# Two layers of a macaron transformer on one core: the last FFN phase is entered from within the second attention

## The chip, the cores and the metric

One core of a Trainium2 chip runs the whole program. The metric is the device time of one execution in microseconds (us), lower is better; the figure compared is the median over executions. TensorE is PE in the profile (its weight loads PEld), VectorE is DVE, ScalarE is ACT, GpSimd is POOL, and SyncE (SP) issues the DMAs.

## The reference

Input x has 2 batches of 1024 tokens of 256 features, all in f32. A "macaron" layer is half an FFN, an attention, half an FFN, each added to x. Layer 0 has 16 heads of 16 with rotary positions, layer 1 has 16 query heads of 128 that share 4 key/value heads; its FFN is six blocks deep.

```
x = x + 0.5 * L0_ffn(norm(x)); x = x + L0_attn(norm(x)); x = x + 0.5 * L0_ffn(norm(x))
x = x + 0.5 * L1_ffn(norm(x)); x = x + L1_attn(norm(x)); x = x + 0.5 * L1_ffn(norm(x))
L1_ffn: six times  x = gelu(x @ W1.T + b1) @ W2.T + b2 + x,  and after each but the last  x = norm(x) * g + b
L1_attn: q, k, v = x @ Wq.T, x @ Wk.T, x @ Wv.T; per head softmax(causal(q @ k.T)) @ v; all heads @ Wo.T + bo
```

## The kernel before

**Precision.** Each f32 operand of a product is kept as a high part (a copy rounded to the matmul type) and a low part (the difference), and a product is three matmuls, low by high, high by low, high by high (`PARTS`). So nearly every tensor is written twice: a high part by ACT (a Copy) and a low part by DVE or POOL (a subtraction); code and text call this a split.

**Phases.** The 2048 tokens are four chunks of 512 (chunks 0 and 1 are batch 0, chunks 2 and 3 are batch 1). Phase 0 is the FFN of layer 0, then comes attention 0, phases 1 and 2 are the two FFNs before attention 1, and phase 3 is the last FFN, six blocks of four chunks. Each engine has its own program, an endless straight order with semaphore waits: an instruction that waits holds up everything behind it on that engine.

**A step of an FFN** is one chunk in one block. For each of eight hidden tiles j, PE does `mm1(j)` (6 matmuls, L291), ACT the gelu (L351) and the high part (L357), DVE the low part (`low(j)`, L462), and PE, three tiles later, `pe_second` (12 matmuls, L316). Beside it DVE takes the former chunk's result (`dve_take`, L388), normalises it (`dve_norm`: statistics L417 and L422, three Newton steps for the inverse root L431 to L434, and the normalised rows `xn` L445), PE turns `xn` (8 transposes, `pe_transpose_chunk`, L277), ACT scales the turned tile and takes its high part (`act_affine`, L337 and L342), DVE its low part (`dve_low_input`, L454), and POOL adds the bias row for the residual (`pool_xb`, L524 to L529). Weights of the next block are loaded into `wraw` and split by quarters, one in each step.

**Attention 1** has 32 head turns (2 batches by 16 heads) in 8 groups of four; groups 0 to 3 are batch 0. The order in a head is a table of words for each engine (`ORDER`, L612): `s6` is the score of query tile 6, `max6` its maximum on DVE (L837), `exp6` its exponential on ACT (L797), `t` the transposes of the probabilities (L732), `high` and `low` the two parts of these (L805, L848), `m` the product with the values (L745), `c` the context, `wo` the output projection (L772) which DVE adds to x (`add_head`, L881). `k`, `v`, `q` are projections (L756); k and v stand only in a group's last head, for the next group. A prime means the next head, a minus the head before. Projections, value transposes and `wo` all use one PSUM bank (`MISC_PS`), in turn: PE fills it, ACT and DVE read it, and only then (`misc_free`) can PE fill it again. Query tiles of one head are all scored before its probabilities for the second half of the keys are turned: `t4` waits for `exp7`.

**Weights of attention 1** lie in HBM in ten pieces for each group. SP loads them into `xb` (L1393, L1397), POOL splits them (`pool_split_a1`, L903 and L905). For the first group this load waits until the FFN before it has written its last input (`xT_ready`).

**Entry into phase 3.** When the last head is added, every engine meets: ACT takes the high parts of the four weight quarters (`entry_high`, L543), DVE and POOL two low parts each (`entry_low`, L548), DVE does the statistics of all 16 token tiles, the Newton steps and the rows of the four chunks in turn; PE turns each, ACT and DVE split each; only then, behind all four chunks in PE's order (`pre_posts`), comes `mm1(0)` of chunk 0.

## Time and profile before

| | |
|---|---|
| median of 3 executions | 2781.11 us (2776.45 to 2782.05) |
| the profiled execution: its own time, its span | 2773.37 us, 2771.5 us |
| busy share of PE, PEld, DVE, ACT, POOL | 91%, 76%, 67%, 51%, 13% |
| granted clock of PE, mean | 0.959 of full |

The busy share says which engine the kernel as a whole leans on. A stage is read from the timeline instead: instructions of one engine in order of time, each line with its start, its length, and in brackets how long the engine had been idle before it and which instruction's end released it.

### The profile page before, as it was taken

What the parts mean: (1) busy time and instruction counts of PE and PEld (TensorE: products, weight loads), DVE (VectorE), ACT (ScalarE), POOL (GpSimd) and SP (SyncE); (2) the same over time, 40 slices, a digit from 0 to 9 for tenths busy, and PEclk for the clock granted to TensorE, in tenths of its full rate; (3) what the DMA queues carried; (4) which work ended last, traced back from release to release, by engine and by line L of the source; (5) the groups of instructions that cost most, each with busy time, mean ns of one, the idle gap of its engine ahead of it and who ended that gap; (6) DMA issues with size and microseconds to landing.
All of it is one profiled execution on the core that took longest, in us unless ns stands there. A gap on an engine that the chain in (4) does not pass through costs nothing. (4 is left out here: it accounts for less than half of the span.)

```text
span 2771.5 us, 49967 instructions
## 1 busy us (share of the span) xinstructions
PE 2532.7 (91%) x16744; PEld 2115.2 (76%) x16744; DVE 1846.5 (67%) x4006; ACT 1399.9 (51%) x2466; POOL 360.4 (13%) x277
## 2 busy tenths in 40 slices
PE   3985989869999999996999999999999599999999
PEld 3863444358888888884887877878878588888888
DVE  4566777457567777764766766767777666777773
ACT  3430555645455555542655555555555455555553
POOL 1000000011122222103000010010000212222220
PEclk9986899979999999997999999999999799999999
DMA  4026133000000000001000000000000000000000
GB/s 155 0 80 141 25 48 47 2 31 31 1 31 31 0 30 30 0 1 38 1 20 1 19 19 0 19 19 0 19 23 9 31 22 9 31 31 0 30 0 31
DMA packets 18925, 73.21 MB, mean 26 GB/s; under 512 B 3328, under 2 KB 8192, under 8 KB 15616
## 3 DMA queue, kind: packets, MB, share of 16 engines
q1 hardware_dynamic: 18816, 71.78, 9.1%
q8 instruction: 66, 1.08, 0.2%
q14 instruction: 43, 0.35, 0.0%
HBM read 61.02 MB, written 10.49 MB: 26 GB/s over the span
## 5 line engine op out<-in xcount | busy, mean ns | idle before, releaser
L316 PEld LDWEIGHTS ps<-w,hid 128*128 128x128 f32 x5376 | 698.9, 191 | 53.6 <-DVE rb L388 15.3
L316 PE MATMUL ps<-w,hid 128*128 128x256 f32 x5376 | 719.2, 284 | 0.6 <-DVE hid L462 0.5
L291 PE MATMUL ps<-xT,w 128*128 (+1 forms) x2688 | 705.7, 399 | 0.0
L462 DVE TENSOR_TENSOR hid<-gel,hid 128x512 fp32r<-128x512 f32 x448 | 397.2, 897 | 368.2 <-ACT hid L357 359.4
L351 ACT ACTIVATE gel<-ps,b 128x512 f32<-128x512 f32 x448 | 306.9, 686 | 560.3 <-issue 547.2
L291 PEld LDWEIGHTS ps<-xT,w 128*128 128x128 f32 x2688 | 481.0, 191 | 79.7
L357 ACT ACTIVATE hid<-gel 128x512 fp32r<-128x512 f32 x448 | 272.8, 622 | 0.0
L745 PE MATMUL ps<-pT,v_sb 128*128 128x512 f32 (+3 forms) x1152 | 260.3, 357 | 1.3 <-DVE pT L848 1.3
L718 PE MATMUL ps<-k_sb,q_sb 128*128 128x512 f32 (+3 forms) x1152 | 251.4, 351 | 1.5 <-DVE q_sb L865 1.4
L837 DVE TENSOR_REDUCE negmax<-ps 128x1 f32<-128x128 f32 (+7 forms) x256 | 192.3, 751 | 78.6 <-PE ps L721 77.5
L1287 DVE TENSOR_REDUCE nmx<-ps 128x1 f32<-128x512 f32 (+3 forms) x384 | 196.0, 552 | 73.0 <-PE ps L1158 55.3
L805 ACT ACTIVATE pT<-ps 128x512 fp32r<-128x512 f32 (+3 forms) x384 | 178.0, 489 | 109.5 <-PE ps L732 109.5
L848 DVE TENSOR_TENSOR pT<-ps,pT 128x512 fp32r<-128x512 f32 (+3 forms) x384 | 205.5, 549 | 24.7 <-ACT pT L805 22.6
L718 PEld LDWEIGHTS ps<-k_sb,q_sb 128*128 128x128 f32 x1152 | 192.6, 190 | 26.8 <-DVE q_sb L865 1.8
L526 POOL TENSOR_TENSOR xb<-xn,rows 128x1024 f32 (+1 forms) x40 | 102.9, 2571 | 791.5 <-DVE xn L445 791.5
L1254 ACT ACTIVATE pT<-ps 128x1024 f32<-128x1024 f32 (+1 forms) x192 | 145.3, 811 | 119.2 <-PE ps L1158 81.9
L756 PE MATMUL ps<-xT,w_a 128*128 (+1 forms) x576 | 162.0, 417 | 44.9 <-DVE k_sb L865 15.4
L745 PEld LDWEIGHTS ps<-pT,v_sb 128*128 128x128 f32 x1152 | 182.7, 189 | 24.7 <-issue 7.3
L454 DVE TENSOR_TENSOR xT<-xTf,xT 128x1024 f32 (+1 forms) x64 | 135.9, 2124 | 86.7 <-ACT xT L342 86.7
L277 PE MATMUL ps<-ident,xn 128*128 128x128 f32 x512 | 82.6, 313 | 117.1 <-DVE xn L445 97.3
L277 PEld LDWEIGHTS ps<-ident,xn 128*128 128x128 f32 x512 | 65.5, 160 | 130.3 <-DVE xn L445 86.6
L797 ACT ACTIVATE p_hi<-ps,negmax 128x640 f32<-128x640 f32 (+3 forms) x128 | 122.4, 956 | 83.3 <-DVE negmax L837 80.9
(111 smaller groups left out, 2909.6 us busy)
## 6 DMA issues: line engine op xcount, KB each, us to landing
wraw<-in_wffn SPq DMA_DIRECT2D x11, 2048.0 KB, 7.8
xb<-in_w_a SPq DMA_DIRECT2D x8, 1280.0 KB, 5.4
qk_dram<-rope_hl SPq DMA_DIRECT2D x16, 512.0 KB, 3.0
xT<-qk_dram SPq DMA_DIRECT2D x60, 128.0 KB, 8.2
xb<-in_wffn SPq DMA_DIRECT2D x3, 2048.0 KB, 10.5
qk_own<-qk_dram SPq DMA_DIRECT2D x36, 128.0 KB, 6.4
x<-in_x SPq DMA_DIRECT2D x4, 512.0 KB, 5.5
rot<-in_rot SPq DMA_DIRECT2D x1, 2048.0 KB, 18.5
```

Source lines behind the costliest of these rows:

```text
L291: last = nc.tensor.matmul(ps[:, HPS + j % 4, :], w[par][:, wp, 0, k * HIDDEN + j * PART:k * HIDDEN + (j + 1) * PART], xT[:, xp, k, bass.ds ...
L316: last = nc.tensor.matmul(y_ps[:, t, :], hid[:, hp, j % 4, t * PART:(t + 1) * PART], w[par][:, wp, 1, j * DIM:(j + 1) * DIM], start=j == 0 ...
L351: nc.scalar.activation(gel[:, j % 4, :], ps[:, HPS + j % 4, :], ACT.Gelu, bias=b1[:, bass.ds((p.tab + blk) * HT + j, 1)]).then_inc(gelu_do ...
L357: nc.scalar.activation(hid[:, 0, j % 4, :], gel[:, j % 4, :], ACT.Copy).then_inc(round_done, 1)
L462: nc.vector.tensor_tensor(hid[:, 1, j % 4, :], gel[:, j % 4, :], hid[:, 0, j % 4, :].bitcast(f32), ALU.subtract).then_inc(low_done, 1)
L718: last = nc.tensor.matmul(dst, q_sb[:, h % 2, qp, q], k_sb[:, kp, k], start=x3 == 0, stop=x3 == 2 and not diagonal)
L745: last = nc.tensor.matmul(ps[:, AV_PS, cols], v_sb[:, vp, kt, :], pT[:, pp, m % PT_SLOTS, cols], start=kt == 0 and n == 0, stop=kt == 3 + ...
L756: last = nc.tensor.matmul(ps[:, MISC_PS, :], a1_piece(wp, which, h, k), xT[:, xp, k, bass.ds(b * SEQ + half * CHUNK, CHUNK)], start=first, ...
L805: nc.scalar.activation(pT[:, 0, m % PT_SLOTS, q0 * PART:], ps[:, T_BANKS[m % 2], q0 * PART:], ACT.Copy).then_inc(pt_high, 1)
L837: nc.vector.tensor_reduce(negmax[:, h % 2, qt:qt + 1], score_view(qt), AX.X, ALU.max, negate=True).then_inc(max_ready, 1)
L848: nc.vector.tensor_tensor(pT[:, 1, m % PT_SLOTS, q0 * PART:], ps[:, T_BANKS[m % 2], q0 * PART:], pT[:, 0, m % PT_SLOTS, q0 * PART:].bitcas ...
L1287: nc.vector.tensor_reduce(nmx[:, g % 2, at:at + 1], src[:, 0:width], AX.X, ALU.max, negate=True)\
```

## The change

1. **Batch 0 enters during the last group.** Groups 4 to 7 only add to batch 1, so chunks 0 and 1 of x are final by then. Their normalisation (8 tiles) is put between DVE's instructions of heads 0 to 2 of the last group (`closing_items`), and their transposes go where the unused `k` words of heads 1 and 2 stand (`transpose_early`, item `n`), through the shared bank: PE 4 transposes, ACT a copy, DVE a subtraction, four times in all. For phase 3's entry there is no scale and shift (they are 1 and 0), so the high part is copied from PSUM at once. A semaphore of its own, `xn_early`, counts the two chunks.
2. **The weights of the first block** are loaded into `wraw` instead of `xb`. ACT takes two quarters before its `high` 10 of the last head and two after the last context; POOL takes all four low parts. PE's first `mm1` waits for two quarters, its first `pe_second` for all.
3. **Batch 1 enters during FFN chunks 0 and 1.** Its statistics, Newton steps and rows (`dve_late_norm`) stand between the `low(j)` of chunk 0, the second chunk's rows in chunk 1; the turns are at the end of chunk 0 and behind `pe_second(0)` of chunk 1. The first block's chunks are written out, not looped. `dve_entry` and `pre_posts` are empty for phase 3.
4. **The weights of attention 1** go through `wraw` too, and the first load waits only for the split of the last weights of phase 2. SBUF is laid out anew for both attentions, with `p_lo` and `p_hi` packed to the triangle that is used, so that `w` of block 0 lies over tensors that are free early.

```diff
+                if p.k == 3 and isinstance(blk, int) and blk == 0:
+                    for c in range(1, CHUNKS):
+                        step(at(blk, c, par, kind), at(blk, c - 1, par, kind))
+                    return
                 with engine.Fori(1, CHUNKS) as c:
...
-            pe.wait_ge(w_split, 4 * (p.n0 + blk + 1))
+            opening = first_block(p, at)
+            if opening and c == 0:
+                pe.wait_ge(w_split, 4 * p.n0 + 2)
+            else:
+                pe.wait_ge(w_split, 4 * (p.n0 + blk + 1))
...
+                if opening and c == 0 and j == LAG:
+                    pe.wait_ge(w_split, 4 * (p.n0 + 1))
                 if j >= LAG:
                     pe_second(pe, at, j - LAG)
                 elif prev is not None:
                     pe_second(pe, prev, HT - LAG + j)
+                if opening and c == 1 and j == LAG:
+                    pe_transpose_chunk(pe, p.s0 - 1)
+            if opening and c == 0:
+                pe_transpose_chunk(pe, p.s0 - 2)
             if prev is not None and prev[5] != "final":
                 pe_transpose_chunk(pe, prev[1])
 
...
+                if first_block(p, at) and (c, j) in ((0, HT), (1, 5)):
+                    act_affine(act, p.s0 - EARLY + c, EARLY + c, 0)
                 if j == HT and prev is not None and prev[5] != "final":
...
+                if not early:
+                    wait(dve, tr_ready, s + chunk)
+                elif chunk:
+                    dve.wait_ge(misc_ready, uses(GROUPS - 1, "n", chunk, 2 * chunk - 1) + 1)
 
                 if not isinstance(xb_made, int) or xb_made > 0:
                     wait(dve, xb_ready, xb_made + chunk)
...
+            parts, late, opening = [], [], first_block(p, at)
+            if opening and c < 2:
+                if c == 0:
+                    late_norm.extend(dve_late_norm(dve, p))
+                late = late_norm[:-1] if c == 0 else late_norm[-1:]
             if prev is not None and prev[5] != "final":
                 parts = dve_norm(dve, prev[1], prev[2], prev[5] == "inner", xb_before(p, prev),
-                                 prev[1] - (CHUNKS - 1) * p.entries)
...
                 low(j)
+                if late and (c == 0 or j == 0):
+                    late.pop(0)()
+                if opening and (c, j) == (1, 5):
+                    dve_low_input(dve, p.s0 - 1, EARLY + 1)
                 if j == 4 and splits_next(p, kind):
                     dve_split(dve, p, at)
                 if j == 1 and prev is not None:
...
         def dve_entry(dve, p):
 
-            if not p.pre:
+            if not p.pre or p.k == 3:
                 return
             s = p.s0 - CHUNKS
...
 
-        def entry_high(act, p):
-            if p.pre:
-                x_ready(act, p.k)
-                act.wait_ge(w_loaded, 16 * (p.n0 + 1))
-                for q in range(4):
-                    nc.scalar.activation(quarter(w[p.n0 % 2][:, 0], q), quarter(xb_raw, q), ACT.Copy).then_inc(w_high, 1)
+        def entry_raw(p):
+            return wraw if p.k == 3 else xb_raw
+
+        def entry_high(act, p, quarters=range(4)):
+            act.wait_ge(w_loaded, 16 * (p.n0 + 1))
+            for q in quarters:
+                nc.scalar.activation(quarter(w[p.n0 % 2][:, 0], q), quarter(entry_raw(p), q), ACT.Copy)\
+                    .then_inc(w_high, 1)
 
...
 
-        def in_order(engine, heads, first=0, last=GROUP):
+        EARLY_AT = (1, 2)
+
+        def in_order(engine, heads, first=0, last=GROUP, closing=None):
 
             todo = []
             for h in heads:
                 for word in ORDER[engine].split():
                     item = word.strip("'-0123456789")
+                    if item == "k" and closing is not None and h - closing in EARLY_AT:
+                        todo.append(("n", h, 2 * (h - closing - EARLY_AT[0]) + int(word.strip("'k"))))
+                        continue
                     head = h + word.count("'") - word.count("-")
                     of_group = {"k": 0, "v": 0, "w": 0}.get(item, head % GROUP)
                     if first <= head < last and head % GROUP == of_group:
...
+            group = [items(e, GROUPS - 1 + over) for over in (-1, 0)]
+            closing = closing_items(e, engine)
+            for item, head, n in in_order(engine, range(GROUP + 1), -1, GROUP, 0):
+                for at in [at for at in closing if at == (item, head, n)]:
+                    closing.pop(at)()
+                group[head // GROUP + 1][item](head % GROUP, n)
+            assert not closing
+
+        def closing_items(e, engine):
+
+            p = phase(3)
+            if engine == "act":
+                return {("high", 3, 10): lambda: entry_high(e, p, (0, 1))}
+            if engine == "dve":
+                norm = dve_early_norm(e, p)
+
+                def begin():
+                    e.wait_ge(misc_free, A1_MISC * (GROUPS - 2))
+                    norm[0]()
+                return {("max", 0, 6): begin, ("max", 0, 7): norm[1], ("low", 0, 3): norm[2], ("low", 0, 6): norm[3],
+                        ("low", 0, 8): norm[4], ("max", 1, 1): norm[5], ("max", 2, 1): norm[6]}
...
+            def transpose_early(h, n):
+                c, k = n // KD, n % KD
+                pe.wait_ge(xn_early, c + 1)
+                wait(pe, misc_free, uses(i1, "n", h, n))
+                for t in range(TPC):
+                    last = nc.tensor.transpose(ps[:, MISC_PS, t * PART:(t + 1) * PART],
+                                               xn[:, t, k * PART:(k + 1) * PART], ident[:])
+                last.then_inc(misc_ready, 1)
+
             def transpose_values(h, r):
...
 
-            return dict(exp=exp, high=high, c=ctx_part,
+            def early(h, n):
+                c, k = n // KD, n % KD
+                act.wait_ge(misc_ready, uses(i1, "n", h, n) + 1)
+                nc.scalar.activation(xT[:, 0, k, c * CHUNK:(c + 1) * CHUNK], ps[:, MISC_PS, :], ACT.Copy)\
+                    .then_inc(misc_high, 1)
...
-            return dict(max=maximum, inv=inverse, low=low, c=ctx_part, v=take_values, wo=add_head,
+            def early(h, n):
+                c, k = n // KD, n % KD
+                cols = slice(c * CHUNK, (c + 1) * CHUNK)
+                dve.wait_ge(misc_high, A1_HIGHS * i1 + HIGHS[which_group(i1)]["n", h, n] + 1)
+                nc.vector.tensor_tensor(xT[:, 1, k, cols], ps[:, MISC_PS, :], xT[:, 0, k, cols].bitcast(f32),
+                                        ALU.subtract).then_inc(misc_free, 1)
...
+
+        a1_raw = wraw_flat.rearrange("p (n e) -> p n e", e=DIM)
 
         def pool_split_a1(pool, i, first):
 
             wait_apart(pool, (w1_loaded, 16 * (i + 1)))
             for piece in range(10):
-                cols = slice(piece * DIM, (piece + 1) * DIM)
+                tile, at = (w_kvq, piece) if piece < 6 else (w_o1, piece - 6)
+                cols = slice(at * DIM, (at + 1) * DIM)
                 if not first:
                     wait_apart(pool, (misc_ready, A1_MISC * (i - 1) + last_use(piece)))
...
                 if k == 3:
-                    sp.wait_ge(xT_ready, S_ATT[1])
-                    sp.dma_start(xb[:, 0:10, :], a["w_a1"][0, :, :].rearrange("p (t e) -> p t e", e=DIM))\
+                    sp.wait_ge(w_split, 4 * p.n0)
+                    sp.dma_start(a1_raw[:, 0:10, :], a["w_a1"][0, :, :].rearrange("p (t e) -> p t e", e=DIM))\
                         .then_inc(w1_loaded, 16)
                     with sp.Fori(1, GROUPS) as i:
...
-                    load(p.n0, p.tab, xb_raw)
+                    load(p.n0, p.tab)
                 if k == 1:
                     load(p.n0 + 1, 1)
...
+                if k == 3:
+                    for c in range(EARLY):
+                        pool.wait_ge(xn_early, c + 1)
+                        pool_residual(pool, c)
                 if p.pre:
-                    entry_low(pool, nc.gpsimd, p, (2, 3) if k == 3 else range(4))
+                    entry_low(pool, nc.gpsimd, p, range(4))
                 if k == 3:
-                    pool.wait_ge(w_split, 4 * (p.n0 + 1))
-                    pre_posts(pool, k, lambda p, s, c: pool_xb(pool, s, c, None, None))
+                    for c in range(EARLY, CHUNKS):
+                        pool_xb(pool, p.s0 - CHUNKS + c, c, None, None)
                 walk(p, pool, lambda at, prev: pool_step(pool, p, at, prev))
                 pool_post(pool, p, tail(p))
...
                     act.wait_ge(xT_ready, S_ATT[1])
                     attention(act, "act", act_att)
-                entry_high(act, p)
+                    act.wait_ge(av_done, 12 * GROUP * GROUPS)
+                    entry_high(act, p, (2, 3))
+                if p.pre and k != 3:
+                    x_ready(act, k)
+                    entry_high(act, p)
                 pre_posts(act, k, lambda p, s, c: act_affine(act, s, c, 0))
```

The order on the engines, at three places.

DVE, head 0 of the last group, from `wo2` of the head before to `low` 2 and 3 (`negmax` is `max6`, then `max7`). Before:

```order
L881 SCALAR_TENSOR_TENSOR x<-ps,rowinv,x 128x256 [waits inv_ready,misc_ready]
L881 SCALAR_TENSOR_TENSOR x<-ps,rowinv,x 128x256
L848 TENSOR_TENSOR pT<-ps,pT 128x512 [waits pt_high]
L837 TENSOR_REDUCE negmax<-ps 128x1 [waits s_ready]
L881 SCALAR_TENSOR_TENSOR x<-ps,rowinv,x 128x256 [waits inv_ready,misc_ready]
L881 SCALAR_TENSOR_TENSOR x<-ps,rowinv,x 128x256
L848 TENSOR_TENSOR pT<-ps,pT 128x384 [waits pt_high]
L837 TENSOR_REDUCE negmax<-ps 128x1 [waits s_ready]
```

With the change, from the same `low` 0 on:

```order
L952 TENSOR_TENSOR pT<-ps,pT 128x512 [waits pt_high]
L452 BN_STATS stats<-x 128x6 [waits misc_free]
L452 BN_STATS stats<-x 128x6 x7
L941 TENSOR_REDUCE negmax<-ps 128x1 [waits s_ready,dve_link,in_loaded]
L985 SCALAR_TENSOR_TENSOR x<-ps,rowinv,x 128x256 [waits inv_ready,misc_ready]
L985 SCALAR_TENSOR_TENSOR x<-ps,rowinv,x 128x256
L952 TENSOR_TENSOR pT<-ps,pT 128x384 [waits pt_high]
L457 BN_AGGR mv<-stats 128x2 x8
L459 TENSOR_SCALAR var<-mv 128x8 [waits dve_link]
L460 TENSOR_SCALAR nt<-var 128x8 [waits dve_link]
L462 TENSOR_SCALAR rstd<-nt 128x8 [waits dve_link]
L941 TENSOR_REDUCE negmax<-ps 128x1 [waits s_ready,dve_link]
```

Eight statistics stand ahead of `max6` and eleven short instructions ahead of `max7`.

PE, head 1 of the last group, from the end of `s7` to the first projection; this is new, before there was nothing between `s7` and `m0` nor between `t3` and `q0`:

```order
L812 MATMUL ps<-mask_b,ident_b 128x128
L857 MATMUL ps<-ident,xn 128x128 [waits misc_free,xn_early]
L857 MATMUL ps<-ident,xn 128x128 x3
L835 MATMUL ps<-pT,v_sb 128x512 [waits ctx_low,pt_low]
L835 MATMUL ps<-pT,v_sb 128x512 x2
L822 MATMUL ps<-ident,p_lo 128x128 [waits pt_low]
L822 MATMUL ps<-ident,p_lo 128x128
L822 MATMUL ps<-ident,p_lo 128x128 [waits pt_low]
L857 MATMUL ps<-ident,xn 128x128 [waits misc_free,xn_early]
L857 MATMUL ps<-ident,xn 128x128 x3
L846 MATMUL ps<-xT,w_kvq 128x512 [waits misc_free,w1_split]
L846 MATMUL ps<-xT,w_kvq 128x512 x5
```

Two fillings of the shared bank come ahead of the projection, each behind a wait for the one before.

PE, from the last `wo` to the first matmuls of phase 3. Before:

```order
L772 MATMUL ps<-w_a,ctxT 128x256 x5
L277 MATMUL ps<-ident,xn 128x128 [waits aff_done,xn_ready]
L277 MATMUL ps<-ident,xn 128x128 x7
L277 MATMUL ps<-ident,xn 128x128 [waits aff_done,xn_ready]
L277 MATMUL ps<-ident,xn 128x128 x7
L277 MATMUL ps<-ident,xn 128x128 [waits aff_done,xn_ready]
L277 MATMUL ps<-ident,xn 128x128 x7
L277 MATMUL ps<-ident,xn 128x128 [waits aff_done,xn_ready]
L277 MATMUL ps<-ident,xn 128x128 x7
L291 MATMUL ps<-xT,w 128x512 [waits gelu_done,xT_ready,w_split]
```

With the change:

```order
L871 MATMUL ps<-w_o,ctxT 128x256 x5
L318 MATMUL ps<-xT,w 128x512 [waits gelu_done,xT_ready,w_split]
L318 MATMUL ps<-xT,w 128x512 x5
L318 MATMUL ps<-xT,w 128x512 [waits gelu_done]
L318 MATMUL ps<-xT,w 128x512 x5
L318 MATMUL ps<-xT,w 128x512 [waits gelu_done]
L318 MATMUL ps<-xT,w 128x512 x5
L318 MATMUL ps<-xT,w 128x512 [waits gelu_done]
L318 MATMUL ps<-xT,w 128x512 x5
L349 MATMUL ps<-w,hid 128x256 [waits y_free,low_done,w_split]
```

The 32 transposes are gone from between the two stages.

## Rows read from the trace of the kernel before

**Rows 1.** Windows: busy us (count) of PE, PEld, DVE, ACT, POOL, PEclk, DMA share, GB/s
```profile
2081.50:2105.10 23.60, 23.60 (x154) 20.50 (x153) 17.98 (x41) 13.94 (x33) 0.00 (x0) 1.00 0.00 1
2030.00:2056.90 26.90, 23.26 (x129) 18.63 (x128) 14.33 (x29) 11.57 (x24) 1.13 (x2) 1.00 0.00 0
2177.60:2193.30 15.70, 7.45 (x32) 6.31 (x33) 9.47 (x15) 7.51 (x9) 8.90 (x4) 0.50 0.11 46
```

**Rows 2.** Timeline of PE at phase 3's entry: start us, length us, instruction [idle before <- releaser]
```profile
2160.77 0.95 PE L772 MATMUL ps<-w_a,ctxT 128*128 128x256 f32 x6 [1.01 <-issue]
...
2193.32 7.64 PE L291 MATMUL ps<-xT,w 128*128 128x512 f32 x24
...
2201.48 1.70 PE L316 MATMUL ps<-w,hid 128*128 128x256 f32 x12 [0.52 <-DVE hid L462]
```

**Rows 3.** Timeline of ACT: weight quarters, the switch to gelu
```profile
2162.67 3.90 ACT L543 ACTIVATE w<-xb 128x1024 fp32r<-128x1024 f32 x4 [4.67 <-DVE x L881]
...
2197.62 1.28 ACT L351 ACT_TABLE_LOAD   x1
...
2198.92 1.26 ACT L351 ACTIVATE gel<-ps,b 128x512 f32<-128x512 f32 x2
```

**Rows 4.** Timeline of POOL at the entry into attention 1
```profile
1282.81 10.23 POOL L1434 TENSOR_TENSOR x<-x,rows 128x1024 f32<-128x1024 f32 x4 [79.84 <-DVE xn L445]
1296.44 0.40 POOL L903 CAST w_a<-xb 128x256 fp32r<-128x256 f32 x1 [3.40 <-DMA xb<-in_w_a]
```

**Rows 5.** Groups by line and form, 2162.6 to 2193.4 us: busy us, mean ns
```profile
L417 DVE BATCH_NORM_STATS2 stats<-x 128x6 f32<-128x256 f32 x16 | 5.3, 410 | 0.0
...
L422 DVE BATCH_NORM_AGGREGATE mv<-stats 128x2 f32<-128x6 f32 x16 | 1.2, 144 | 0.0
```

**Rows 6.** Timeline of DVE and POOL in the entry
```profile
2165.69 4.64 POOL L548 TENSOR_TENSOR w<-xb,w 128x1024 fp32r<-128x1024 f32 x2 [92.40 <-ACT w L543]
2168.08 4.47 DVE L548 TENSOR_TENSOR w<-xb,w 128x1024 fp32r<-128x1024 f32 x2
...
2174.29 0.17 DVE L431 TENSOR_TENSOR nt<-rstd 128x16 f32<-128x16 f32 x1
...
2176.18 1.38 DVE L445 TENSOR_SCALAR xn<-x,mv,rstd 128x256 f32<-128x256 f32 x4
```

**Rows 7.** Timeline of PE, DVE and ACT, head 0 of the last group: max6, s7's end, max7, exp7, t4
```profile
2071.31 1.08 DVE L837 TENSOR_REDUCE negmax<-ps 128x1 f32<-128x896 f32 x1
...
2073.17 0.23 PE L721 MATMUL ps<-mask_b,ident_b 128*128 128x128 bf16 x1
...
2073.56 1.21 DVE L837 TENSOR_REDUCE negmax<-ps 128x1 f32<-128x1024 f32 x1
...
2074.85 1.12 ACT L797 ACTIVATE p_hi<-ps,negmax 128x1024 f32<-128x1024 f32 x1
...
2076.89 1.06 PE L732 MATMUL ps<-ident,p_hi 128*128 128x128 f32 x8
```

**Rows 8.** Timeline of ACT and PE: the shared bank from a fill's end to the next; four transposes
```profile
2043.21 0.60 ACT L826 ACTIVATE k_sb<-ps 128x512 fp32r<-128x512 f32 x1 [1.30 <-PE ps L756]
...
2044.59 1.66 PE L756 MATMUL ps<-xT,w_a 128*128 x6 [1.41 <-DVE k_sb L865]
...
2062.33 0.60 PE L765 MATMUL ps<-ident,xTf 128*128 128x128 f32 x4
```

**Rows 9.** Timeline of ACT at the end of the last head: high10, the last context
```profile
2154.72 0.39 ACT L805 ACTIVATE pT<-ps 128x256 fp32r<-128x256 f32 x1 [0.43 <-PE ps L732]
...
2157.40 0.60 ACT L814 ACTIVATE ctxT<-ps 128x512 fp32r<-128x512 f32 x1 [1.59 <-PE ps L745]
```

**Rows 10.** Timeline of PE in phase 3: a step's end with its 8 transposes
```profile
2237.35 1.09 PE L277 MATMUL ps<-ident,xn 128*128 128x128 f32 x8
2238.20 1.64 PE L291 MATMUL ps<-xT,w 128*128 x6
```

**Rows 11.** DMA issues, 2000 to 2300 us: count, KB each, median us to landing
```profile
wraw<-in_wffn SPq DMA_DIRECT2D x2, 2048.0 KB, 7.8
```

127 lines of the change are left out of this document (76 added, 51 removed).

## The prediction

> **What bounds the kernel now.** I read the page first, then the windows. In a plain head of attention 1 PE is busy for the whole of its 23.6 us while DVE works 18.0 and ACT 13.9 of them [rows 1]: in there PE sets the time, and DVE has some 5.6 us of idle time in a head. The seam between attention 1 and phase 3 is different. The PE timeline shows the last `wo` ending at 2160.77 + 0.95 = 2161.72 and the first `mm1` at 2193.32 [rows 2]: 31.6 us in which PE does nothing but 32 transposes. In the second half of that seam PE's granted clock is 0.50, which is 1.2 GHz of 2.4 [rows 1], after PE had stood still from 2161.72 on. The clock is still recovering when `mm1` starts, and `pe_second` follows 8.16 us later [rows 2]. A second, smaller seam lies at the entry into attention 1: POOL ends its bias sums at 1282.81 + 10.23 = 1293.04, then idles 3.40 us for the weights' DMA, and PE's first projection waits for the split behind it [rows 4].
>
> **The change, part by part.** All is set against the profiled execution (2773.4 us, of which the span is 2771.5); its time is 7.7 us under the median, and I take the same difference off the median.
>
> *Removed, the seam: 31.6 us.* PE's order goes from the last `wo` straight to `mm1(0)`. What it waits for: two weight quarters. ACT's four quarters took 3.90 us, 0.98 each [rows 3]; POOL's subtraction is 4.64 / 2 = 2.32 each [rows 6]. ACT starts them ahead of `high10`, at about 2154.3, so POOL has two done at about 2155.3 + 4.6 = 2160, before the last `wo` ends; the last two are done some 2.9 us after 2161.72, and `pe_second(0)` wants them 5.8 us after it. So this wait costs nothing; without that cover it would cost up to 4.6.
>
> *Removed, the slow start: 2.1 us.* The chain before `pe_second(0)` is one `mm1` (1.64, rows 10 show such a six), then from the table load to the product 2201.48 - 2197.62 = 3.86 us [rows 2, 3], 5.5 together. Four `mm1` at full clock are about as long. I take 5.8, and 0.3 more because the statistics of batch 1 (8 x 0.33 = 2.7) now stand between `low(0)` and `low(1)`: 8.16 - 6.1 = 2.1. The rows put the gelu 1.30 us behind the start of the table load [rows 3]. The Trainium skill (ScalarE: Activation LUTs, What ACT_TABLE_LOAD costs) adds a drain of about 1.38 us to a load of 1.28; the trace does not show that drain, and by the page the opening would be 1.4 us longer and the whole gain smaller by as much.
>
> *Removed at the entry of attention 1: 3.4 us.* The DMA is issued a block earlier, so POOL's 3.40 us of idle time [rows 4] go. Everything behind (k projection, value projection) only moves forward.
>
> *Added in head 0 of the last group: 3.8 us.* Ahead of `max6` and `max7` DVE gets 2.7 (8 statistics, 5.3 / 16 each) and 8 x 0.08 + 3 x 0.21 = 1.2 [rows 5]; 0.21 is the pitch of a short instruction, (2176.18 - 2174.29) / 9 for the nine of the Newton steps [rows 6]. DVE runs without a gap there, and `t4` on PE waits for `exp7`, which waits for `max7`: `exp7` ends at 2075.97, `t4` starts at 2076.89, so the cover is 0.9 [rows 7]. 3.9 - 0.9 = 3.0 reach PE. The first Newton step (0.6) and the later `exp7` push the low part of q's first half, and the second half waits for the shared bank: 0.8 more. PE has no slack in a head [rows 1], so nothing of this is made up later.
>
> *Added, the early turns: 3.8 us in each of heads 1 and 2, 7.6 together.* The bank's turnaround, from ACT's copy to the next filling, is 2044.59 - 2043.21 = 1.38, and four transposes take 0.60 [rows 8]. Two turns are 2 x (0.60 + 1.38) = 4.0 behind the end of `s7`. On DVE both stand ahead of `max7`, on ACT ahead of `exp6` and `exp7`. So `exp7` ends about 4.0 + 1.2 + 1.3, with hand-overs some 6.9, behind the end of `s7`, and `t4` about 7.3 behind it; before it was 2076.89 - 2073.40 = 3.5 [rows 7]. That the stretch with k and v has the same chain and shows PE busy 23.3 of 26.9 us [rows 1] speaks for stalls of this kind.
>
> *Added, Newton steps 2 and 3 and the rows: 2.5 us.* On DVE 2 x 0.6 and 2 x 1.38 [rows 6] make 4.0. They stand near idle time of DVE; I let 2.5 reach PE.
>
> *Added at the end of the last head: 0.7 us.* Two quarters (1.95) stand ahead of `high10`. ACT was idle 0.43 before it and 1.59 before the last context [rows 9], which hides most of it.
>
> *Moved into the FFN: 2.2 us.* 16 transposes in two lots of 8, 1.09 each lot [rows 10], on PE, where nothing covers them. The statistics, Newton steps, rows and two low inputs of batch 1 are about 2.7 + 1.2 + 1.9 + 2.8 and two subtractions of 1.2 (the second of L548's, rows 6: 4.47 less the wait behind POOL) on DVE, over two chunks; `low(j)` is wanted three tiles after `mm1(j)`, and I cost them at nothing beyond the 0.3 above. SP's load of block 1's weights is issued when POOL is done and lands 7.8 us later [rows 11], about when ACT's split in chunk 0 asks for it; a microsecond of lateness there is hidden by the three-tile lag. POOL's two early bias sums (some 2.6 each, 10.23 / 4, rows 4) run beside attention and are awaited by nobody.
>
> Sum: 31.6 + 2.1 + 3.4 = 37.1 less 3.8 + 7.6 + 2.5 + 0.7 + 2.2 = 16.8 is a gain of **20.3 us**: 2753.1 for the profiled execution, **2761** for the median. Bounds of the costs: below, only the turns' own PE time (4 x 0.60) and the 2.2, so 4.6 and a gain of 32.5 (2749). Above, four bank turns at 2.0, all DVE work of the early norm (2.7 + 1.2 + 1.9 + 2.8), 2.0 for ACT's quarters, 2.2, and 6.3 for an opening that is late on POOL and the DMA: 27 and a gain of 10 (2771). I take the middle because the order puts the pieces ahead of `max6`, `max7`, where DVE has no gap.
>
> **Rivals.**
>
> *The norm hides (2754.5).* DVE idles 5.6 us in a head [rows 1] and its 8.6 us of early norm are spread over three heads. If all of it hides, 3.8 + 2.5 = 6.3 less is paid. For it: the idle share. Against: DVE's idle time lies elsewhere in the head, not between `max5` and `low3`. 15%.
>
> *POOL stands in DVE's way at the opening (2768).* The row of the seam shows it: DVE's two weight subtractions started at 2168.08 and took 4.47, while POOL ran two until 2170.33 [rows 6]. The first DVE one lasted as long as POOL's, the second 1.2. With the change POOL subtracts four quarters, 9.3 us, and makes two bias sums of 2.6 in the first two chunks, beside DVE's `low(j)`, which also reads two SBUF tensors. If the last quarter reaches into `low(0)` (2.3) and both sums hold `low(j)` up to PE (2 x 2.6), the opening costs 7.5 us more. For: the row. Against: POOL should be done 2 us before `low(0)`, which comes some 4.9 us after 2161.72, and `low(j)` has the three-tile lag. The Trainium skill (SBUF — State Buffer, SBUF: two separate sides) has the rule: a DVE op with two SBUF inputs and a GpSimd op that reads SBUF take one port pair in turn, for the whole instruction. The row agrees. 12%.
>
> *Half clock in the last group (slower, up to 2807).* PE granted 0.50 after it had stood still [rows 1]. The change puts waits of 1 to 4 us into a group that had none. Each microsecond at 1.2 GHz costs half of one, so the gain is gone when over 40.6 us of the last group (some 92, not quite four heads of 23.6) run at half clock, and if all do it is 46 - 20 = 26 slower. Against: the stretch with k and v has stalls of up to 1.4 us and shows 1.00 [rows 1, 8]. 3%.
>
> *The seam is only shifted (no change).* If the early turns or the last weight quarter came so late that PE stood still for some 20 us again, somewhere between the last `wo` and chunk 1. The weights' load is issued when POOL has split the last group's weights, early in that group, and no instruction that is moved is that long. 2%.
>
> **How the numbers follow.** The forecast has 68%. The likeliest is 2761. The range goes from the lower bound of the costs, 2749, to 2770, which takes in the late opening; it leaves out the clock and the shifted seam and the outermost runs. A measurement of this kernel tells about 0.2% (5.6 us) from no change: faster by more than that is 68 + 15 + 12 = 95%, within it 2%, slower 3%.
>
> **What would show it.** In the profile of the changed kernel: (1) the last `wo` and the first `mm1` less than 1 us apart, `pe_second` 5.5 to 6.5 us later at a granted clock of 1.00; (2) POOL's first split of attention 1 right behind its bias sums; (3) the last group about 14.6 us longer than its 92, in three lots: idle time of PE before L822 and L846 (`t4`, projections) in heads 0, 1 and 2; (4) steps of chunks 0 and 1 as long as the others but for 1.1 us of transposes. The forecast is wrong if the last group grows by under 8 or over 20 us, if PE waits for `w_split` at the seam, or if chunk 0 or 1 takes over 3 us more than chunk 2.

## The result, and the profile after

The changed kernel takes 2767.69 us (median of 12 executions, 2751.26 to 2780.14) beside 2779.18 us (12, 2771.89 to 2792.64): a ratio of 0.9943 (interval 0.9918 to 0.9967), or some 16 us less (9 to 23); the two medians themselves are 11.5 us apart. It is faster, and 2767.69 lies in the range of the prediction, 2749 to 2770, 6.7 us above its number. The profiled execution took 2771.37 us (span 2769.5, mean granted clock 0.956), only 2.0 less than that of before. The two timelines, laid side by side from the start, tell why:

| stretch, PE's timeline | before | after | difference |
|---|---|---|---|
| start to the last transposes ahead of attention 1 | 1282.79 | 1299.23 | +16.44 |
| from there to the first projection | 15.00 | 11.53 | -3.47 |
| groups 0 to 6 | 770.34 | 770.44 | +0.10 |
| last group: heads 0, 1, 2 | 23.71, 23.61, 23.61 | 28.39, 27.52, 27.06 | +4.68, +3.91, +3.45 |
| head 3, to the end of the last `wo` | 22.66 | 23.83 | +1.17 |
| last `wo` to the first `pe_second` | 39.76 | 6.23 | -33.53 |
| from there to the end | 570.02 | 575.27 | +5.25 |

All that the change touches gives -18.44 us. The first line arises in attention 0, of which the change moves only the place in memory: PE's first product of its heads starts at 227.2 and 227.8 us, and its last output projection ends at 565.7 and 582.1. Experiments 10 to 12 are about it. In the windows (columns as in [rows 1]) of the last group's four heads and of the opening:

```profile
2081.20:2109.60 28.40, 25.94 (x155) 22.03 (x155) 24.43 (x74) 13.79 (x33) 3.51 (x3) 0.94 0.20 75
2109.60:2137.10 27.50, 25.26 (x162) 21.58 (x162) 20.40 (x47) 14.93 (x35) 2.39 (x1) 1.00 0.00 1
2137.10:2164.20 27.10, 25.10 (x163) 21.55 (x163) 19.31 (x43) 15.07 (x35) 0.00 (x0) 1.00 0.00 1
2164.20:2188.00 23.80, 19.81 (x125) 16.87 (x124) 15.49 (x37) 13.98 (x26) 7.58 (x4) 0.96 0.00 1
2188.00:2194.20 6.20, 6.20 (x25) 4.72 (x24) 1.64 (x4) 3.96 (x6) 1.79 (x1) 0.88 0.53 172
```

Where a head was all PE [rows 1], PE now stands still for 2.0 to 2.5 us in each of heads 0 to 2. The timelines of DVE, ACT and PE show how it comes about in head 0, where [rows 7] had no gap:

```profile
2084.39 2.70 DVE L452 BATCH_NORM_STATS2 stats<-x 128x6 f32<-128x256 f32 x8
2087.18 1.09 DVE L941 TENSOR_REDUCE negmax<-ps 128x1 f32<-128x896 f32 x1
...
2088.97 0.55 DVE L952 TENSOR_TENSOR pT<-ps,pT 128x384 fp32r<-128x384 f32 x1
...
2088.31 1.01 ACT L895 ACTIVATE p_hi<-ps,negmax 128x896 f32<-128x896 f32 x1 [4.12 <-DVE negmax L941]
...
2089.58 0.33 PE L822 MATMUL ps<-ident,p_lo 128*128 128x128 f32 x1 [2.12 <-DVE pT L952]
2089.68 2.16 PE L846 MATMUL ps<-xT,w_kvq 128*128 128x512 f32 x6
```

The statistics push `max6`, for which ACT waits 4.12 us, and everything behind it on DVE. PE's 2.12 us are for `low1` (L952), which stands behind the statistics, `max6` and an addition of `wo3`; ACT had its high part long before (2083.71 to 2084.19). The six matmuls behind take 2.16 us where they take 1.64 at full clock. In head 1 PE waits in the turns themselves, for the one shared bank (L857 is the early turn):

```profile
2116.81 0.63 PE L857 MATMUL ps<-ident,xn 128*128 128x128 f32 x4 [0.49 <-DVE xT L994]
2118.94 1.64 PE L846 MATMUL ps<-xT,w_kvq 128*128 128x512 f32 x6 [1.50 <-DVE xT L994]
```

Then the seam. [Rows 2] had 31.6 us here; now the FFN's first product stands right behind the last `wo`:

```profile
2186.38 1.62 PE L871 MATMUL ps<-w_o,ctxT 128*128 128x256 f32 x6 [1.01 <-issue]
2187.80 6.56 PE L318 MATMUL ps<-xT,w 128*128 128x512 f32 x24
2194.23 1.66 PE L349 MATMUL ps<-w,hid 128*128 128x256 f32 x12
```

That last `wo` took 0.95 before and takes 1.62 now. The windows show a granted clock of 0.53, which is nearly all at the lower level (0.5, 1.2 GHz), and before it PE busy for 0.90 and 0.98 of 2 us:

```profile
2182.00:2184.00 2.00, 0.90 (x6) 0.76 (x6) 0.64 (x4) 0.98 (x2) 2.00 (x2) 1.00 0.00 0
2184.00:2186.00 2.00, 0.98 (x6) 0.77 (x6) 1.00 (x4) 1.50 (x2) 2.00 (x2) 1.00 0.00 0
2186.00:2188.00 2.00, 1.62 (x7) 1.65 (x8) 0.28 (x1) 0.00 (x0) 2.00 (x2) 0.53 0.00 0
2188.00:2190.00 2.00, 2.00 (x8) 1.52 (x7) 0.88 (x2) 0.00 (x0) 1.79 (x1) 0.62 0.00 0
```

Last, chunk 1 of the FFN, in the timelines of DVE, POOL and PE: beside POOL's sum of 2.40 us DVE's low part takes 2.25 and not 0.69, DVE's take (L423) is late, and PE waits for it; at the chunk's end it waits again, for the norm's rows. The last three lines are the first `mm1` of chunks 1, 2 and 3: chunk 1 takes 28.01 us, chunk 2 23.75.

```profile
2217.03 2.25 DVE L500 TENSOR_TENSOR hid<-gel,hid 128x512 fp32r<-128x512 f32 x1 [0.84 <-ACT hid L390]
2219.21 1.27 DVE L423 TENSOR_TENSOR rb<-ps,xb 128x512 f32<-128x512 f32 x2
...
2216.33 2.40 POOL L568 TENSOR_TENSOR xb<-xn,rows 128x1024 f32<-128x1024 f32 x1 [6.98 <-DVE xn L483]
...
2220.03 1.67 PE L349 MATMUL ps<-w,hid 128*128 128x256 f32 x12 [1.50 <-DVE rb L423]
...
2235.56 1.09 PE L300 MATMUL ps<-ident,xn 128*128 128x128 f32 x8 [1.66 <-DVE xn L483]
...
2208.40 1.65 PE L318 MATMUL ps<-xT,w 128*128 128x512 f32 x6
...
2236.41 1.65 PE L318 MATMUL ps<-xT,w 128*128 128x512 f32 x6
...
2260.16 1.65 PE L318 MATMUL ps<-xT,w 128*128 128x512 f32 x6
```

### The profile page after: what moved, and what is told of

It is laid out like the page before. It is cut to its first block and busy times, and to the rows that moved or that the text cites. A ratio compares the mean times of both kernels' runs of the same rounds, so it can differ in the third digit from the quotient of the medians.

```text
span 2769.5 us, 49771 instructions
## 1 busy us (share of the span) xinstructions
PE 2550.3 (92%) x16744; PEld 2123.4 (77%) x16744; DVE 1843.1 (67%) x4018; ACT 1396.5 (50%) x2464; POOL 367.1 (13%) x279
## 5 line engine op out<-in xcount | busy, mean ns | idle before, releaser
L952 DVE TENSOR_TENSOR pT<-ps,pT 128x512 fp32r<-128x512 f32 (+3 forms) x384 | 205.8, 550 | 24.7 <-ACT pT L903 22.7
L809 PEld LDWEIGHTS ps<-k_sb,q_sb 128*128 128x128 f32 x1152 | 192.8, 190 | 26.8 <-DVE q_sb L969 1.8
L846 PE MATMUL ps<-xT,w_kvq 128*128 (+1 forms) x576 | 162.6, 418 | 44.5 <-DVE k_sb L969 15.3
L492 DVE TENSOR_TENSOR xT<-xTf,xT 128x1024 f32 (+1 forms) x62 | 128.9, 2079 | 80.1 <-ACT xT L375 80.1
L300 PE MATMUL ps<-ident,xn 128*128 128x128 f32 x496 | 76.9, 305 | 94.3 <-DVE xn L483 81.0
L846 PEld LDWEIGHTS ps<-xT,w_kvq 128*128 128x128 f32 x576 | 103.7, 193 | 77.1 <-issue 36.1
```

Source lines behind the costliest of these rows:

```text
L809: last = nc.tensor.matmul(dst, q_sb[:, h % 2, qp, q], k_sb[:, kp, k], start=x3 == 0, stop=x3 == 2 and not diagonal)
L846: last = nc.tensor.matmul(ps[:, MISC_PS, :], a1_piece(wp, which, h, k), xT[:, xp, k, bass.ds(b * SEQ + half * CHUNK, CHUNK)], start=first, ...
L952: nc.vector.tensor_tensor(pT[:, 1, m % PT_SLOTS, q0 * PART:], ps[:, T_BANKS[m % 2], q0 * PART:], pT[:, 0, m % PT_SLOTS, q0 * PART:].bitcas ...
```

## The experiments

Each is read by the same stretches as above: the four heads of the last group, from `t0` to `t0` on PE (head 3 to the end of the last `wo`), from `t0` of head 3 to the first `pe_second`, and from there to the end. All times in us, one profile each.

| kernel | heads 0, 1, 2, 3 | `t0` of 3 to `pe_second` | to the end |
|---|---|---|---|
| before | 23.71, 23.61, 23.61, 22.66 | 62.42 | 570.02 |
| changed | 28.39, 27.52, 27.06, 23.83 | 30.06 | 575.27 |
| 1 turns at vacant places | 28.23, 23.61, 24.43, 24.34 | 30.72 | 575.01 |
| 2 norm spread | 23.83, 23.62, 28.46, 29.33 | 36.33 | 574.51 |
| 3 both | 23.66, 23.60, 24.43, 24.10 | 30.74 | 574.83 |
| 4 load late | 28.22, 28.91, 27.06, 23.82 | 30.11 | 575.07 |
| 5 late rows | 28.51, 27.51, 27.06, 23.84 | 30.11 | 573.83 |
| 6 no sums | 28.43, 27.50, 27.08, 23.83 | 30.07 | 573.44 |
| 7 quarters last | 28.42, 27.53, 27.07, 23.10 | 32.25 | 575.43 |
| 8 end filled | 28.41, 27.50, 27.06, 22.82 | 25.46 | 578.15 |
| 9 all moves | 23.68, 23.62, 24.42, 24.14 | 26.77 | 572.62 |
| 10 before, again | 23.68, 23.62, 23.59, 22.64 | 62.41 | 570.01 |
| 11 all moves, again | 23.67, 23.61, 24.44, 24.15 | 26.78 | 572.53 |
| 12 changed, again | 28.22, 28.94, 27.06, 23.86 | 29.95 | 575.00 |

**1. The turns at vacant places.**

```diff
-        EARLY_AT = (1, 2)
+        EARLY_AT = dict(pe={(2, "w0'"): 0, (2, "w1'"): 1, (3, "q1'"): 2, (3, "w0'"): 3},
+                        act={(3, "w0"): 0, (3, "w1"): 1, (3, "q1'"): 2, (4, "w0"): 3})
+        EARLY_AT["dve"] = {(3, "w0"): 0, (3, "w1"): 1, (4, "q1"): 2, (4, "w0"): 3}
...
-                        ("low", 0, 8): norm[4], ("max", 1, 1): norm[5], ("max", 2, 1): norm[6]}
+                        ("low", 0, 8): norm[4], ("max", 1, 1): norm[5], ("inv", 3, 0): norm[6]}
```

> The changed kernel, with the four early turns of batch 0 taken out of the places of k0' and k1' in heads 1 and 2 (ahead of exp6 and max7) and put where the shared bank has a vacant place: w0' and w1' ahead of head 3, q1' and w0' in head 3. The norm's DVE pieces stay where they were, only the second rows stand later, in head 3. In the changed kernel the last group takes 106.8 us from the first t0 to the end of the last wo, and its heads are 4.7, 3.9, 3.5 and 1.2 longer than before. Theory A (the place costs): the turns are dear because exp7 and t4 of their head wait for two bank turnarounds in a row; at vacant places only PE's own 4 x 0.6 = 2.4 us is paid, heads 1 and 2 lose some 5.5 us together, and the last group takes 101 us. Theory B (the work costs, wherever it stands: four fillings of the shared bank of 1.4 and more): the last group stays at 106 to 107.5 us and the cost moves to head 3.

Measured: the last group takes 100.6 us (101 expected by A, 106 by B). Head 1 is a plain head again, though the first rows still stand just before it. Heads 2 and 3 pay 0.8 and 0.5 for what PE itself does in the turns. Times: 0.9916 of before (0.9884 to 0.9949).

**2. The norm where DVE is idle.**

```diff
-        EARLY_AT = (1, 2)
+        EARLY_AT = (2, 3)
...
-                return {("max", 0, 6): begin, ("max", 0, 7): norm[1], ("low", 0, 3): norm[2], ("low", 0, 6): norm[3],
-                        ("low", 0, 8): norm[4], ("max", 1, 1): norm[5], ("max", 2, 1): norm[6]}
+                return {("max", 0, 4): begin, ("q", 1, 0): norm[1], ("max", 1, 4): more_variance,
+                        ("q", 2, 0): norm[3], ("max", 2, 4): both, ("max", 3, 4): norm[5]}
```

> The changed kernel, with the early norm of batch 0 cut into lots of at most 2.0 us, each put where the trace of before shows DVE idle: ahead of max4 (2.13 idle there, 1.53 in head 0) and of q0' (0.94), spread over all four heads; the turns stay at the places of k0' and k1', but in heads 2 and 3, as the norm is done later. Theory A (the place costs): the 4.7 us of head 0 go nearly (0.5 left), head 1 is a plain head plus 0.5, head 2 carries the turns as head 1 did (3.9), head 3 has no q projections and pays some 3 us for its turns; the last group takes 101 to 102 us in place of 106.8. Theory B (DVE's 8.6 us of added work cost wherever they stand): 106 us or more.

Measured: head 0 is 23.83, 0.1 over before's, and head 1 23.62: what stands of the norm in these two heads is hidden. That is A, but the group takes 105.2 and not 101 to 102, since heads 2 and 3, to which the turns moved, are 4.9 and 6.7 longer than before's (with half clock in both, and in head 3 the weight quarters of experiment 7). In head 3 PE has no q projections to do meanwhile, so it waits for ACT and DVE, and then gets half clock (timeline and window):

```profile
2162.68 0.91 PE L854 MATMUL ps<-pT,v_sb 128*128 128x256 f32 x6 [2.35 <-DVE pT L971]
```
```profile
2164.00:2168.00 4.00, 3.44 (x15) 2.65 (x14) 2.06 (x3) 1.42 (x3) 0.00 (x0) 0.51 0.00 0
```

Had only the total been looked at (-1.6 us), theory B (106 or more) would have seemed nearly right; the heads one by one say the reverse. Times: 0.9919 (0.9889 to 0.9948).

**3. Both.** The edits of 1 and 2 together, with the norm's last pieces ahead of `q0'` in head 2 and of `inv0` in head 3.

> Both moves together: the norm's pieces ahead of max4 and q0', the turns at the vacant places of w0', w1' ahead of head 3 and of q1', w0' in head 3. Theory A (the place costs, and the two costs are independent, so they add): PE pays its own 2.4 us of transposes, the end with its 1.2 us and about 1 us of leftovers, so the last group takes 97.5 to 99 us against 106.8, and the kernel is some 8 us faster than the changed one, 24 faster than before. Theory B (the work costs): 105 us or more.

Measured: 95.8 us, 2.2 over before's 93.6 and 1.7 under the lowest that was expected. It saves 11.0 us, more than experiments 1 and 2 together (6.2 and 1.6), as the turns no longer meet the places that made them dear in 2. Of the 2.2, PE's own part of a turn is some 0.4 (head 2 with two of them is 0.82 longer), less than the 0.6 of its row, and 0.36 is half clock in the last `wo` (1.31 against 0.95 in [rows 2]). These are all the idle times of PE in the group; only the 0.30 ahead of a turn (L874, for the shared bank) has no counterpart in the kernel before:

```profile
2138.22 0.91 PE L852 MATMUL ps<-pT,v_sb 128*128 128x256 f32 x6 [0.30 <-DVE pT L969]
2141.14 1.00 PE L852 MATMUL ps<-pT,v_sb 128*128 128x512 f32 x3 [0.59 <-DVE pT L969]
2147.93 0.63 PE L874 MATMUL ps<-ident,xn 128*128 128x128 f32 x4 [0.30 <-DVE x L1002]
2151.84 0.96 PE L888 MATMUL ps<-w_o,ctxT 128*128 128x256 f32 x6 [1.41 <-DVE ctxT L977]
2153.82 1.31 PE L888 MATMUL ps<-w_o,ctxT 128*128 128x256 f32 x6 [1.01 <-issue]
```

So of 13.2 us some 11 were the places; the 2.2 left are the work and that half clock. Times: 0.9897 (0.9874 to 0.9920).

**4. The first load late.**

```diff
-                    sp.wait_ge(w_split, 4 * p.n0)
+                    sp.wait_ge(xT_ready, S_ATT[1])
                     sp.dma_start(a1_raw[:, 0:10, :], a["w_a1"][0, :, :].rearrange("p (t e) -> p t e", e=DIM))\
```

> The changed kernel, but the weights of attention 1's first group are loaded as before, after xT of the phase is ready, and not a block earlier. Theory A (the term of 3.4 in the prediction): POOL stands idle some 3.4 us behind its bias sums again, and from the start of the last transposes ahead of attention 1 to the first projection it is 15.0 us in place of 11.5. Rival (the 3.5 us gained there come from the new place of the weights in the memory, since w_kvq now lies elsewhere and a1_raw is read in place of xb): it stays at 11.5 us.

Measured: 1312.54 to 1327.38, 14.84 us, with POOL's idle time back; so the term is the load. POOL's timeline, to set beside [rows 4]:

```profile
1312.56 10.22 POOL L1548 TENSOR_TENSOR x<-x,rows 128x1024 f32<-128x1024 f32 x4 [79.97 <-DVE xn L483]
1326.04 0.40 POOL L1017 CAST w_kvq<-wraw 128x256 fp32r<-128x256 f32 x1 [3.26 <-DMA wraw<-in_w_a]
```

Its times, 0.9915 (0.9893 to 0.9937), are no higher than the changed kernel's: executions differ too much for a term of 3 us, which only the timeline shows.

**5. The late rows behind the take**, and **6. POOL's sums cut short** (from 1024 columns to 8; this kernel leaves out most of the residual and bias of chunks 2 and 3).

```diff
-                if late and (c == 0 or j == 0):
+                if late and c == 0:
                     late.pop(0)()
...
                     dve_take(dve, p, prev)
+                    if late:
+                        late.pop(0)()
```

> The changed kernel, but in chunk 1 DVE makes the second half of the late rows behind its take of chunk 0's output and not ahead of low(1). In the changed kernel it is 575.3 us from the first pe_second to the end of the span, 5.2 more than before; a sum of POOL (2.40 us) that is released by these rows runs beside DVE's low(1), which took 2.25 us in place of 0.69, the take is late, and PE waits 1.50 us for it. Theory A (it is the place): the stall of 1.5 goes and the stretch takes 573.7 us. Theory B (the sum then meets the next low(j) and the wait only moves): 575.0 to 575.5 us.

```diff
+                nc.gpsimd.tensor_tensor(xb[:, bass.ds(c * TPC, 1), 0:8], xn[:, 0:1, 0:8], rows[:, B2_1:B2_1 + 1, 0:8],
+                                        ALU.add).then_inc(xb_ready, 1)
```

> The changed kernel with POOL's two bias sums of batch 1 (chunks 2 and 3 of the FFN's first block) cut from 1024 columns to 8, so the residual and bias of these chunks are left out; all instructions and waits stay. Theory A (POOL and DVE take turns at SBUF): low(j) beside them takes 0.69 us and not 2.25 and 2.85, the stall of 1.50 us ahead of pe_second in chunk 1 goes, and the stretch from the first pe_second to the end takes 573 to 573.8 us against 575.3. Rival (DVE's own added norm work or the two lots of transposes make all of the 5.2): 575.0 us or more, and low(j) is as slow as in the changed kernel.

Measured: 573.83 and 573.44, both by A. With the rows behind the take, low(1) and the take (L423) are on time; with POOL's sum at 0.20 us they are so too, in the old order:

```profile
2221.95 0.69 DVE L500 TENSOR_TENSOR hid<-gel,hid 128x512 fp32r<-128x512 f32 x1 [2.13 <-ACT hid L390]
2222.56 1.28 DVE L423 TENSOR_TENSOR rb<-ps,xb 128x512 f32<-128x512 f32 x2
```
```profile
2210.75 0.69 DVE L500 TENSOR_TENSOR hid<-gel,hid 128x512 fp32r<-128x512 f32 x1 [0.84 <-ACT hid L390]
2211.36 1.28 DVE L423 TENSOR_TENSOR rb<-ps,xb 128x512 f32<-128x512 f32 x2
...
2210.05 0.20 POOL L582 TENSOR_TENSOR xb<-xn,rows 128x8 f32<-128x8 f32 x1 [9.16 <-DVE xn L483]
```

So the sum beside the low part made the 1.5 us: moving the rows that release it gets 1.4 us back, removing both sums 1.8. (The 2.85 us of the expectation are a row of two low parts, beside the first sum; no wait of PE came of them.)

**7. All quarters last.**

```diff
-                return {("high", 3, 10): lambda: entry_high(e, p, (0, 1))}
...
-                    entry_high(act, p, (2, 3))
+                    entry_high(act, p)
```

> The changed kernel with all four weight quarters on ACT behind the last context of attention 1 and none ahead of high10. By the prediction's term the two quarters ahead of high10 cost 0.7 us at the end of the last head: without them head 3 takes 23.1 us in place of 23.8; but POOL has its second quarter only some 5.7 us behind ACT's start, so that the first mm1 waits 1.4 us for it, and from the start of t0 in head 3 to the first pe_second it is 30.5 to 31.5 us against 30.06. Rival (the quarters hide fully behind ACT's idle time): head 3 stays at 23.8 us and the first mm1 comes 1.4 us or more later.

Measured: head 3 takes 23.10 us, 0.73 less, the size of the prediction's term (0.7). But the first `mm1` waits 1.59 us for POOL's second quarter, and the four behind it take 7.72 us and not 6.56:

```profile
2191.51 7.72 PE L318 MATMUL ps<-xT,w 128*128 128x512 f32 x24 [1.59 <-POOL w L607]
```
```profile
2190.00:2192.00 2.00, 0.49 (x1) 0.49 (x2) 0.83 (x2) 0.00 (x0) 2.00 (x2) 0.50 0.00 0
2192.00:2194.00 2.00, 2.00 (x6) 1.52 (x6) 0.00 (x0) 0.00 (x0) 2.00 (x2) 0.50 0.00 0
```

`pe_second` comes at 32.25 us, 0.75 over the highest expected: the half clock was left out of that sum. To place two quarters early costs 0.7 and saves 2.9.

**8. The end filled.**

```diff
+                return {("wo", 3, 2): first_tile, ("wo", 3, 3): lambda: pe_first(e, at, 1)}
...
-                return {("high", 3, 10): lambda: entry_high(e, p, (0, 1))}
+                return {("high", 3, 6): lambda: entry_high(e, p, (0, 1))}
```

> The changed kernel, with mm1(0) and mm1(1) of the FFN's first chunk put on PE ahead of the last two wo of attention 1, and ACT's first two weight quarters ahead of high6, where ACT was idle 1.78 us. In the changed kernel PE is idle 1.41 and 1.01 us ahead of these wo, the granted clock falls to 0.53 and 0.62 from 2186 to 2190, and from the start of t0 in head 3 to the first pe_second it is 30.06 us. Theory A (the clock falls because PE's work thins out there): both idle times and the half clock go, 26.0 to 26.8 us. Theory B (the clock falls for another reason): only the idle times go, 27.4 to 27.9 us, with half clock somewhere in the stretch. Theory C (the quarters ahead of high6 hold up the products): 28.5 us or more, with PE waiting for pT in head 3.

Measured: 25.46 us, better than A's 26.0 to 26.8. PE has no gap at the end, the clock is 1.00 throughout, and the last `wo` takes 0.88. But the FFN behind it grew by 2.9 us, to 578.15, which no theory had: of the 4.6 us 1.7 are left. PE and ACT in chunk 0 (L625 splits the next block's weights), first the last `wo`:

```profile
2181.03 0.88 PE L884 MATMUL ps<-w_o,ctxT 128*128 128x256 f32 x6
...
2195.84 1.70 PE L354 MATMUL ps<-w,hid 128*128 128x256 f32 x12 [2.07 <-DVE hid L505]
...
2192.84 1.06 ACT L625 ACTIVATE w<-wraw 128x1024 fp32r<-128x1024 f32 x1 [6.83 <-issue]
```

ACT stands 6.83 us ahead of that split, with the gelus queued behind it: the load is issued at 2184.07, when POOL is done with the buffer (2179.08 + 4.77 = 2183.85), and takes 8.7 us. In the changed kernel ACT waited 2.30 us at the same place, which the three-tile lag hid; the earlier first `pe_second` uncovered it:

```profile
2197.95 1.06 ACT L620 ACTIVATE w<-wraw 128x1024 fp32r<-128x1024 f32 x1 [2.30 <-issue]
```

**9. All moves in one**, with that split later:

```diff
-                if j == 3 and splits_next(p, kind):
+                if j == (6 if first_block(p, at) and c == 0 else 3) and splits_next(p, kind):
                     act_split(act, p, at)
...
-                if j == 4 and splits_next(p, kind):
+                if j == (7 if opening and c == 0 else 4) and splits_next(p, kind):
                     dve_split(dve, p, at)
...
-                if opening and (c, j) == (1, 5):
+                if opening and (c, j) == (1, 6):
                     dve_low_input(dve, p.s0 - 1, EARLY + 1)
```

> All that paid so far in one kernel: norm pieces ahead of max4 and q0', turns at the vacant places, mm1(0) and mm1(1) ahead of the last two wo with the quarters ahead of high6, late rows behind the take; and, new, in the opening chunk ACT's and DVE's split of block 1's weights behind gelu(6) and low(7) and not behind gelu(3) and low(4), and the low input of chunk 3 one step later in chunk 1. In the run with the filled end ACT stood 6.83 us ahead of that split, for the load, and PE waited 2.07 us for low(j). If these savings add up: t0 of head 0 to first pe_second 97.5 to 98.5 us (133.4 before, 113.0 in the changed kernel), first pe_second to the end 572.0 to 573.0 us (570.0 before, 575.3 in the changed kernel, 578.2 with the filled end alone), no wait of PE for low(j) over 0.5 us in chunk 0. From the last transposes ahead of attention 1 to the end 1452 to 1453.5 us against 1470.3 in the changed kernel and 1488.7 before. Rival (the splits moved late hold up gelu(7) and chunk 1, or the shared bank is short where turns and wo meet): 1456 us or more.

Measured: `t0` of head 0 to `pe_second` 98.5 us, from there 572.6, and 1452.9 from the last transposes to the end, all as expected. PE's idle times from 2150 to the FFN's last step are 0.20, 0.30, 0.26 and 0.53 us. What is left over before is 2.3 us in the last group and 2.6 in the FFN, of these 1.6 for the two lots of transposes (below) and 0.8 for the last two waits.

**10. The kernel before again**, with nothing changed, for the first line of the table of stretches.

> The kernel before, unchanged, profiled once more. The last transposes ahead of attention 1 began at 1282.8 us in its first profile, and at 1299.2, 1295.0, 1294.2, 1277.5, 1312.5, 1304.6, 1293.0, 1301.7 and 1294.1 in profiles of the changed kernel and its variants. Theory A (attention 0's half clock differs from execution to execution, whatever the kernel): the kernel before also begins them somewhere between 1277 and 1313, and not again within 1 us of 1282.8. Theory B (the new memory layout of attention 0 made it some 13 us longer): 1281 to 1285, as in its first profile.

Measured: 1289.80 us, as by A, 7.0 later than in its first profile, while all that follows repeats within 0.1 (groups 0 to 6 770.31, the FFN 570.01). In the windows of attention 0 the granted clock differs, here of before, of the same kernel again, of the changed one, of the changed one again (experiment 12), and of the kernel with all moves again (experiment 11):

```profile
280.00:560.00 280.00, 249.30 (x2528) 125.42 (x2526) 185.16 (x424) 156.62 (x221) 0.00 (x0) 0.90 0.22 30
```
```profile
280.00:560.00 280.00, 252.93 (x2502) 125.24 (x2501) 181.52 (x415) 154.41 (x217) 0.00 (x0) 0.87 0.23 30
```
```profile
280.00:560.00 280.00, 255.03 (x2421) 128.17 (x2423) 182.25 (x416) 147.71 (x207) 0.00 (x0) 0.83 0.22 30
```
```profile
280.00:560.00 280.00, 247.80 (x2561) 127.52 (x2562) 186.46 (x427) 156.45 (x221) 0.00 (x0) 0.93 0.23 30
```
```profile
280.00:560.00 280.00, 249.14 (x2527) 125.36 (x2525) 184.89 (x424) 156.62 (x221) 0.00 (x0) 0.90 0.23 30
```

The starts are 1282.8, 1289.8, 1299.2, 1279.3 and 1282.8, in the order of the clock.

**11 and 12. The kernel with all moves, and the changed one, timed together.**

> The kernel with all moves again, now timed against the kernel before. By the one profile of each, its stretch from the last transposes ahead of attention 1 to the end is 35.8 us shorter than before (1452.9 against 1488.7). Theory A (attention 0 spreads alike for all kernels, and nothing else differs): a ratio of about 0.987 (0.984 to 0.990), 2746 to 2750 us beside 2781 to 2784. Rival (part of it comes back as half clock in attention 0, in the way the changed kernel's gain of 18.4 us by the same sum showed as 11 to 16 in its times): 0.990 to 0.993.

> The changed kernel, unchanged, timed against the kernel before on the same chip. The sum over the profiles from attention 1 on is 18.4 us. Theory A (the times fell short of it, 0.9943, since attention 0 happened to spend more time at half clock in those runs): 0.9925 to 0.9950, and its profile begins the last transposes ahead of attention 1 elsewhere than at 1299.2 us, while the stretch behind is again 1470.3 us within 1. Rival (the new memory layout costs in attention 0 in every run): that start is again between 1295 and 1303, and the ratio is 0.9945 or above.

Measured, beside 2781.04 us of before (16 executions): the changed kernel 2762.97 (11), ratio 0.9932 (0.9902 to 0.9962); with all moves 2743.95 (6), ratio 0.9853 (0.9815 to 0.9892), some 41 us less than before (30 to 51; the medians are 37 apart) and faster than both. Both ratios are in the range of their theory A. The stretch from the last transposes to the end is 1453.0 with all moves, as in experiment 9. In the second profile of the changed kernel the last transposes start at 1279.25, 20 us earlier than in the first, and the stretch behind them is 2749.1 - 1279.25 = 1469.9, as against 1470.3. So the new memory layout is not what made attention 0 long. At the same clock the two layouts take the same time: experiment 11 has the new one and starts its last transposes at 1282.84, the kernel before at 1282.79, both with 0.90 in the window. That the layout has no part in how often the lower clock comes isn't shown: the old layout in the changed kernel wasn't tried.

## Why the prediction was right, and where not

The number came out in the range, and most terms hold in size; in two of them the wait that counts was another than the working has, and one of its own signs of being wrong came true (FFN, below).

**Seam, 31.6: right.** PE goes from the last `wo` into `mm1` with no gap, and it never waits for `w_split`.

**Slow start, 2.1: nearly.** 6.43 us from `mm1` to `pe_second` (5.5 to 6.5 forecast), so 1.7. PE has no gap in it: the four `mm1` make the time. The granted clock was forecast at 1.00 all through and was 0.53 to 0.62 until 2190. The gelu follows the start of the table load by 1.30 us again (2190.22 to 2191.52). The drain of about 1.38 us that the Trainium skill adds (ScalarE: Activation LUTs, What ACT_TABLE_LOAD costs) does not show after the change either.

**Entry of attention 1, 3.4: right,** 3.47, and shown by experiment 4.

**Head 0, 3.8: near in size, on another path.** 4.68; experiment 2 takes the norm away from there and 4.56 go. The step has `t4` wait for `exp7`, with 0.9 of cover. What PE waits for is the low parts ahead of `t4` in its own order: 2.12 us for `low1`, which stands behind the statistics on DVE, and in experiment 12, where head 0 has full clock, 0.50 and 0.18 more for the next two. The half clock costs little here: head 0 takes 28.22 there and 28.39 with it.

**Turns, 3.8 each: right in size.** 3.91 and 3.45. Experiment 1 takes them away and head 1 is plain. But the wait is PE's own for the shared bank, ahead of the second turn and of the projection (0.49 and 1.50 in head 1), and not `t4` for `exp7`: `exp7` ends at 2121.08 and `t4` starts, with no idle time before it, at 2121.60.

**Newton steps and rows, 2.5: too dear.** PE's waits for the low part behind the two lots of rows are 0.34 and 0.24 us, 0.6 together, and lie within the 4.68 and 3.91 above:

```profile
2104.45 0.33 PE L822 MATMUL ps<-ident,p_hi 128*128 128x128 f32 x1 [0.34 <-DVE pT L952]
...
2131.98 0.33 PE L822 MATMUL ps<-ident,p_hi 128*128 128x128 f32 x1 [0.24 <-DVE pT L952]
```

The step said that they stand near idle time of DVE, and did not look it up place by place.

**End of the last head, 0.7: about right.** Experiment 7 takes the quarters away and 0.73 go, some 0.2 of it half clock: the last `wo` takes 1.62 us in the changed kernel, 1.41 there, and 0.95 before. So the head's 1.17 are about 0.5 for the quarters and 0.7 for half clock, which goes where the end is filled (experiments 8 and 9).

**FFN, 2.2: mis-sized, 5.25.** "I cost them at nothing" is the sentence that failed, for DVE's late norm in chunks 0 and 1, and the sign that the forecast set for it came true: chunk 1 takes 4.3 us more than chunk 2, over the 3 it allowed. The transposes were priced too high: PE goes on 0.79 us after each late lot starts (2207.61 to 2208.40, and 2221.54 to 2222.33), 1.6 together. The rival on POOL had the mechanism, priced at 7.5: its late quarter did not occur, and of the two sums only one reached PE, with 1.5 us (experiments 5 and 6). That its number, 2768, is the nearest to the measured median is chance. The rule of the Trainium skill on the two sides of SBUF (SBUF — State Buffer, SBUF: two separate sides) is what rows show here: 2.25 us beside POOL's sum, 0.69 without it. Then come the 1.66 us at the end of chunk 1. There DVE's low input of chunk 3 (2232.40 to 2233.62) stands ahead of the norm's last Newton step and rows; in experiment 9, with it a step later among other moves, 0.26 and 0.53 are left of the waits for rows. It was not moved alone, so this cause is argued. The transposes, these two waits and one of 0.31 us in chunk 0 make 5.1 of the 5.25.

**The sum:** 37.0 gained (33.5 at the seam, 3.5 at the entry) and 18.6 paid (13.2 in the last group, where 14.6 were forecast; 5.25 in the FFN, 2.2 forecast; 0.1 in groups 0 to 6), where 37.1 and 16.8 were forecast. That is 18.4 against 20.3: the FFN took 3.0 more, the last group gave 1.4 back. The two timings, 0.9943 and 0.9932, are 16 and 19 us by the ratios, 11 and 18 by the medians. The executions of a kernel spread by 20 us and more with attention 0's clock, so that the median lies 6.7 us above the forecast, and not 1.9, tells nothing of the change.

**The rivals.** "The norm hides" did not come true for the change as made, and is true where the norm is put ahead of `max4` (experiment 2); its argument was right that the idle share is there, and so was the objection that it lies elsewhere. "Half clock in the last group" came true in small: 0.2 us in head 0 and 0.7 in the last `wo` of the changed kernel, 1.4 in head 1 of experiment 12 (below). Its price is too low: at half clock the six matmuls of a projection take 2.85 us (experiment 12, 2097.51) and 1.64 at full, so a group of 92 us would take up to 92 more, and not 46. Nothing here came near that.

## What to carry to other kernels

Idle time of an engine is worth what it is at the place where work is put: the same pieces cost 13.2 us ahead of `max6` and `max7` and behind `s7`, and 2.2 at places that the timeline shows vacant, so look up each piece's place by the brackets, not by a head's share. Price a moved step by what is queued behind it on every engine, and when one wait goes, ask which one it covered (here a load that was 2.3 us late unseen, and cost 2.1 when PE came 4.6 us earlier). Where a part that the change doesn't touch spreads by 20 us from run to run, compare the stretches behind it in the traces; those mostly repeat within 0.5 us, and terms of 3 us can be told that the times can't tell.

## What the runs showed of the hardware that was not expected

**Attention 0's clock differs from execution to execution.** The start of the last transposes ahead of attention 1 lay between 1277.5 and 1312.5 us in fourteen profiles, with mean granted clocks from 0.93 down to 0.79 over 280 to 560 us, and in all but two neighbours of the fourteen a later start goes with a lower clock. Of the 20.4 us by which the two profiled spans of the changed kernel differ (2769.5 and 2749.1), 20.0 lie ahead of that start. In experiment 4 it reached into attention 1, whose groups 0 to 6 took 775.8 us in place of 770.3. Why the clock is granted differently with the same instructions stays open.

**Half clock can follow waits of some 2 us, for a few microseconds.** After PE had been busy 2.46 of 4 us, the clock was 0.69 and 0.88 in the next two windows of head 0:

```profile
2085.00:2089.00 4.00, 2.46 (x13) 1.59 (x11) 3.91 (x11) 0.69 (x1) 1.13 (x2) 1.00 0.45 115
2089.00:2093.00 4.00, 3.42 (x12) 2.96 (x13) 3.76 (x20) 1.97 (x6) 0.00 (x0) 0.69 0.95 406
2093.00:2097.00 4.00, 4.00 (x25) 3.50 (x24) 2.92 (x9) 2.85 (x7) 0.00 (x0) 0.88 0.01 4
```

In experiment 12 head 0 had waits just as long (2.17 of 4 us busy) with a clock of 1.00, and the half clock came in head 1, which took 28.94 us in place of 27.52. So where it falls is not told by the waits alone; why stays open. At the end of the last head it was there in the changed kernel and gone in experiment 8, where PE had something to do; so filling gaps of 2.4 us, with the quarters where ACT was idle, gave back 4.6.
